# A routed expert layer on one core: the first tile of each expert shrinks from 256 to 128 rows and uses raw fp32 weights

## The reference, cut to what matters

```python
g = jnp.einsum('bsh,ih->bsi', x, gw)
u = jnp.einsum('bsh,ih->bsi', x, uw)
return jnp.einsum('bsi,hi->bsh', jax.nn.silu(g) * u, dw)
...
bids = confidences * wealth
top_bids, selected_experts = jax.lax.top_k(bids, K)      # K = 2 of E = 8
...
x = x + jnp.tanh(g_ffn[0]) * _L0_ffn_ref(_layernorm(x, axis=-1), ...)
```

| expert | 0 | 1 | 2 | 3 | 4 | 5 | 6 | 7 |
|---|---|---|---|---|---|---|---|---|
| rows | 1 | 1 | 272 | 1 | 3820 | 1 | 3 | 4093 |

## Time and profile before

### The profile page before, as it was taken

One profiled execution on the slowest core, in us unless ns is written; L12 is line 12 of the kernel. 1 busy time (PEld: TensorE's weight loads), 2 busy tenths in 40 slices (PEclk: granted clock), 3 DMA queues, 4 the chain that ended last, 5 costly groups with the idle time before them and its releaser, 6 DMA issues.

```text
span 1313.1 us, 25666 instructions
## 1 busy us (share of the span) xinstructions
PE 1158.8 (88%) x9261; PEld 1021.7 (78%) x9261; DVE 672.9 (51%) x1536; ACT 552.5 (42%) x863; POOL 361.3 (28%) x385
## 2 busy tenths in 40 slices
PE   5789888888888888618897999999997999999995
PEld 4556666666666665418897999999997999999995
DVE  2546666666666665445756444444456444444442
ACT  3456565566555554424544232323334323232331
POOL 2112333344334331223534211111133111111111
PEclk7789998999899997758998999999998999999998
DMA  9000111011011100135535321211223222111121
GB/s 319 15 10 26 35 34 33 33 33 38 33 34 42 38 33 27 42 117 200 155 93 157 87 33 29 33 29 24 33 34 114 34 33 33 29 32 30 24 33 24
DMA packets 50753, 73.46 MB, mean 56 GB/s; under 512 B 6288, under 2 KB 42384, under 8 KB 50576
## 3 DMA queue, kind: packets, MB, share of 16 engines
q0 software_dynamic: 20544, 44.05, 14.2%
q1 hardware_dynamic: 29072, 27.65, 7.0%
q10 hardware_dynamic: 1088, 1.11, 0.3%
HBM read 47.11 MB, written 25.43 MB: 55 GB/s over the span
## 4 chain that ended last, share of the span: by engine, by line
PE 44%; DVE 5%; issue 3%; ACT 2%; DMA 1%; POOL 0%; DVEq 0%; POOLq 0%; ACTq 0%
PE gate L1213 15%; PE up L1213 15%; PE down L1229 14%; DVE w_lo L104 4%; ACT h_hi L1273 1%; PE turned L1202 1%; DVE h L1299 1%; ACT w_hi L99 1%; DMA stage<-up_T 1%; DMA out<-y,token 0%; DVE x_lo L1291 0%; DVE h_lo L1301 0%; POOL out L1348 0%; POOL stage L86 0%; DVE y L1314 0%
## 5 line engine op out<-in xcount | busy, mean ns | idle before, releaser
L1348 POOL DMA_INDIRECT out<-y,token x76 | 119.6, 1573 | 495.8 <-DVE y L1314 364.8
L1268 ACT ACTIVATE silu<-gate 128x512 f32<-128x512 f32 x152 | 90.6, 596 | 334.3 <-PE up L1213 334.3
L1299 DVE TENSOR_TENSOR h<-silu,up 128x512 f32<-128x512 f32 x152 | 104.2, 686 | 220.0 <-ACT silu L1268 220.0
L1229 PE MATMUL down<-w_hi,h_hi 128*128 128x256 f32 x608 | 176.4, 290 | 18.4 <-DVE h_lo L1301 18.2
L873 DVE TENSOR_REDUCE max_neg<-maxps 128x4 f32<-128x1024 f32 x128 | 156.4, 1222 | 60.7 <-PE maxps L487 59.1
L1301 DVE TENSOR_TENSOR h_lo<-h,h_hi 128x512 fp32r<-128x512 f32 x152 | 117.9, 776 | 109.6 <-ACT h_hi L1273 109.6
L1229 PE MATMUL down<-w_hi,h_lo 128*128 128x256 f32 x608 | 171.8, 283 | 0.0
L1229 PE MATMUL down<-w_lo,h_hi 128*128 128x256 f32 x608 | 171.5, 282 | 0.0
L675 ACT ACTIVATE probs<-scores 128x1024 f32<-128x1024 f32 x128 | 132.0, 1032 | 90.4 <-PE scores L506 90.3
L1273 ACT ACTIVATE h_hi<-h 128x512 fp32r<-128x512 f32 x152 | 96.0, 631 | 128.7 <-DVE h L1299 128.1
L1213 PE MATMUL gate<-x_hi,w_hi 128*128 128x256 f32 x608 | 125.0, 288 | 12.4 <-issue 7.9
(11 more groups left out here) (153 smaller groups left out, 2162.6 us busy)
## 6 DMA issues: line engine op xcount, KB each, us to landing
xg<-dispatched SPq DMA_DIRECT2D x39, 272.0 KB, 2.8
stage<-gate_T POOLq DMA_DIRECT2D x8, 1024.0 KB, 5.5
stage<-up_T POOLq DMA_DIRECT2D x8, 1024.0 KB, 7.1
stage<-down_T POOLq DMA_DIRECT2D x8, 1024.0 KB, 6.3
x_all<-x SPq DMA_DIRECT2D x16, 256.0 KB, 4.6
ctxT<-ctxT SPq DMA_DIRECT2D x16, 256.0 KB, 2.7
out<-x_all SPq DMA_DIRECT2D x16, 256.0 KB, 2.1
out<-y,token POOLq DMA_INDIRECT x76, 3.8
```

Of the source, the lines that this page charges most:

```text
L1229: last = mm(down[t][:, 0:D], r[:, i, t * P:(t + 1) * P], weights(par, w, 2)[:, i, :], start=i == 0 and m == 0, stop=i == IC - 1 and m == 2)
L1268: nc.scalar.activation(silu[pair % 2][:], gate[pair % 2][:], ACT.Silu).then_inc(s_silu, 1)
L1299: V.tensor_tensor(h[pair % 2][:], silu[pair % 2][:], up[pair % 2][:], ALU.mult).then_inc(s_made, 1)
L1348: pool.indirect_dma_start(out, bass.IndirectOffsetOnAxis(token[:, t:t + 1], axis=0), y[:, t, :], None, compute_op=ALU.add).then_inc(s_adde ...
```

## The change

Each expert's first tile now has 128 rows (`FIRST`) instead of 256, and uses the raw fp32 weights as they land. The tokens are the stationary operand: 8 matmuls of 128 rows by 512 inner columns give `gate` and `up`, two calls of SiLU and two of the product give `h` with rows on partitions, eight transposes (`flip`) and two copies by ScalarE (`hT`) turn it, and 8 matmuls of 256 columns contract it. These are plain fp32 matmuls with one term in place of three. The remaining rows of an expert go through `rest`, tiles of 256 rows with the split weights as before, and their number is now (rows + 127) // 256, which can be 0.

The weights that are split during an expert's first tile are now its *own*, six halves on ScalarE and all six on VectorE, whether or not a `rest` tile follows. There is one pair `w_hi`, `w_lo` instead of two, and three raw buffers instead of one; GpSimd loads the weights of two experts ahead and computes nothing any more. A third of the weights is laid out on the host so that each partition reads one contiguous piece.

```diff
+        def load_third(eng, e, n, to):
+            of = (gate_T, up_T, down_T)[n][e]
+            eng.dma_start(to[:, n * third:(n + 1) * third], of).then_inc(s_stage[e % STAGES][n], 16)
...
-            link(V.tensor_single_scalar(tiles[:], tiles[:], TILE.bit_length() - 1, ALU.arith_shift_right))
-            V.tensor_scalar(tiles[:], tiles[:], 1, None, ALU.max).then_inc(s["counted"], 1)
+            link(V.tensor_scalar(tiles[:], EPILOGUE2.bank("COUNT")[:, 0, 0:EXPERTS], float(TILE - 1 - FIRST), None, ALU.add))
+            V.tensor_single_scalar(tiles[:], tiles[:], TILE.bit_length() - 1, ALU.arith_shift_right).then_inc(s["counted"], 1)
...
+        def over_tiles(eng, name, first, rest, before_rest=None):
+            r = eng.alloc_register(name)
+            eng.reg_mov(r, 0)
             for e in range(EXPERTS):
-                if before_expert:
-                    before_expert(e)
-                tile(e, 0, eng.snap(n), True)
-                eng.reg_add(n, n, 1)
-                count = eng.value_load(tiles[0:1, e:e + 1], min_val=1, max_val=TOKENS // TILE)
-                with eng.If(count > 1):
-                    with eng.Fori(1, count) as j:
-                        tile(e, j, eng.snap(n), False)
-                        eng.reg_add(n, n, 1)
-            return eng.snap(n)
+                before = None if e == 0 else eng.snap(r)
+                first(e, before, 0 if e == 0 else before + e)
+                count = eng.value_load(tiles[0:1, e:e + 1], min_val=0, max_val=TOKENS // TILE)
+                with eng.If(count > 0):
+                    if before_rest:
+                        before_rest(e)
+                    with eng.Fori(0, count) as j:
+                        done = eng.snap(r)
+                        rest(e, j, done, done + (e + 1))
+                        eng.reg_add(r, r, 1)
+            return eng.snap(r)
```

```diff
+            def before_rest(e):
+                for n in range(3):
                     pe.wait_ge(s_split[n], 2 * (e + 1))
...
+            def first_gate_up(e, half, n):
...
+                w = stages[e % STAGES]
+                for mat, bank in ((0, gate[half]), (1, up[half])):
+                    if half == 0:
+                        wait_stage(pe, e, mat)
+                    for c in range(HC):
+                        last = mm(bank[:].rearrange("p a b -> p (a b)"), x_full[:, c, :],
+                                  weights(w, mat)[:, c, half * (INNER // 2):(half + 1) * (INNER // 2)],
+                                  start=c == 0, stop=c == HC - 1)
+                last.then_inc(s_pair, 2)
...
+            def first(e, r, n):
+                pe.wait_ge(s_xlo, n + 1)
+                first_gate_up(e, 0, n)
+                first_gate_up(e, 1, n)
+                flip_h(e, 0, n)
+                turn_rows(n * 16 + 32)
+                wait_stage(pe, e, 2)
+                if not is_zero(n):
+                    pe.wait_ge(s_y, n * TT)
+                first_contract(e, 0, (0, 1))
+                flip_h(e, 1, n)
+                first_contract(e, 0, (2, 3))
+                first_contract(e, 1, range(IC // 2)).then_inc(s_down, 1)
...
             def high_of_rows(done):
                 act.wait_ge(s_turned, done)
+                nc.scalar.activation(x_full[:], turned[:, :, 0:FIRST], ACT.Copy)
                 nc.scalar.activation(x_hi[:], turned[:], ACT.Copy).then_inc(s_xhi, 1)
```

```diff
+                round_weights(*HALVES[:3])
+                first_silu(0)
+                if not is_zero(n):
+                    act.wait_ge(s_down, n)
+                round_weights(*HALVES[3:5])
+                first_silu(1)
+                read_flip(0)
+                round_weights(*HALVES[5:])
+                read_flip(1)
+                high_of_rows(n + 2)
...
+                note_rows(e)
+                rest_of_weights(*HALVES[:2])
+                first_h(0)
+                rest_of_weights(*HALVES[2:4])
+                first_h(1)
+                rest_of_weights(*HALVES[4:])
+                next_rows(r, n, e)
+                V.tensor_scalar(y[:, 0, :], down[0][:, 0:D], weight[:, 0:1], None, ALU.mult).then_inc(s_y, TT)
...
-            def prepare_weights(e):
-                for half in range(2 if e > 0 else 1):
-                    rest_of_weights(pool, e, 0, half, hi[e % 2], lo[e % 2])
-                if e + 1 < EXPERTS:
-                    for n in range(3):
-                        pool.wait_ge(s_split[n], 2 * (e + 1))
-                        load_third(pool, e + 1, n)
...
+            def wait_added(firsts, r, t=0):
...
+            def load_weights(e):
+                for n in range(3):
+                    load_third(pool, e, n, stages[e % STAGES])
+            for e in range(1, STAGES):
+                load_weights(e)
+            def first(e, r, n):
+                if 0 < e and e + STAGES - 1 < EXPERTS:
+                    alone.wait_ge(s_down, n)
+                    for m in range(3):
+                        pool.wait_ge(s_split[m], 2 * e)
+                    load_weights(e + STAGES - 1)
+                pool.wait_ge(s_y, n * TT + TT)
+                if e > 0:
+                    wait_added(e, r)
+                pool.indirect_dma_start(out, bass.IndirectOffsetOnAxis(token[:, 0:1], axis=0),
```

More of the change, by code:

```diff
@@ L73, in build_program @@
         tiles = sb(keep, "tiles", [P, EXPERTS], i32)
-        s_stage = [sem(f"stage_loaded{n}") for n in range(3)]
+        s_stage = [[sem(f"stage{b}_loaded{n}") for n in range(3)] for b in range(STAGES)]
         s_split = [sem(f"weights_split{n}") for n in range(3)]
@@ L1107, in _, with expert_stage @@
             pool.wait_ge(s["scattered"], BATCHES * 16 * 2 * QT)
-def expert_stage(nc, sb_in, sem, load_third, round_weights, rest_of_weights, disp, out, idn, tiles, s_split, s_padded, ROUNDED):
+def expert_stage(nc, sb_in, sem, load_third, disp, out, idn, tiles, stage, s_stage, s_hi, s_split, s_padded):
     with ExitStack() as own:
@@ L1113, in sb @@
             return sb_in(own, name, shape, dt)
-        hi = [sb(f"w_hi{i}", [P, WCOLS], f32r) for i in range(2)]
-        lo = [sb(f"w_lo{i}", [P, WCOLS], f32r) for i in range(2)]
+        stages = [stage] + [sb(f"stage{i}", [P, WCOLS]) for i in range(1, STAGES)]
+        hi = sb("w_hi", [P, WCOLS], f32r)
+        lo = sb("w_lo", [P, WCOLS], f32r)
         xg = sb("xg", [P, TT, ROW])
@@ L1123, in expert_stage @@
         h_lo = sb("h_lo", [P, IC, TILE], f32r)
+        hT = [sb(f"hT{i}", [P, IC // 2, FIRST]) for i in range(2)]
         weight = sb("weight", [P, TT])
@@ L1134, in expert_stage @@
         down = [own.enter_context(nc.psum_tensor(f"down{i}", [P, 512], fp32)) for i in range(TT)]
+        flip = own.enter_context(nc.psum_tensor("flip", [P, IC // 2, FIRST], fp32))
         s_rows = sem("rows_loaded")
@@ L1243, in tile @@
                 turn_rows(n * 16 + 32)
-                contract(e, 2, n, first)
-                contract(e, 3, n, first)
-            def gate_up_split(e):
-                for n in range(2):
+                contract(2, r, n)
+                contract(3, r, n)
+            def before_rest(e):
+                for n in range(3):
                     pe.wait_ge(s_split[n], 2 * (e + 1))
+            def first_gate_up(e, half, n):
+                pe.wait_ge(s_made, n * PAIRS + (half + 1))
+                w = stages[e % STAGES]
[7 more added lines that the diff above has]
+                last.then_inc(s_pair, 2)
@@ new lines, in flip_h, with first_contract @@
+            def flip_h(e, half, n):
+                pe.wait_ge(s_made, n * PAIRS + (2 * half + 4))
+                if 2 * e + half > 0:
+                    pe.wait_ge(s_flipped, 2 * e + half)
+                for i in range(IC // 2):
+                    last = nc.tensor.transpose(flip[:, i, :], h[half][:].rearrange("p a b -> p (a b)")[:, i * P:(i + 1) * P], idn[:])
+                last.then_inc(s_flip, 1)
+            def first_contract(e, half, pieces):
+                pe.wait_ge(s_flipped, 2 * e + half + 1)
+                w = weights(stages[e % STAGES], 2)
+                for i in pieces:
+                    at = half * (IC // 2) + i
+                    last = mm(down[0][:, 0:D], hT[half][:, i, :], w[:, at, :], start=at == 0, stop=at == IC - 1)
+                return last
@@ L1251, in _ @@
             turn_rows(16)
-            over_tiles(pe, "pe_count", tile, gate_up_split)
+            over_tiles(pe, "pe_count", first, rest, before_rest)
         @block.scalar
@@ L1257, in high_of_rows, with rest @@
                 act.wait_ge(s_turned, done)
+                nc.scalar.activation(x_full[:], turned[:, :, 0:FIRST], ACT.Copy)
                 nc.scalar.activation(x_hi[:], turned[:], ACT.Copy).then_inc(s_xhi, 1)
-            def tile(e, j, n, first):
-                def next_weights(n, half):
-                    if first and e + 1 < EXPERTS:
-                        round_weights(act, e + 1, n, half, hi[(e + 1) % 2])
+            def rest(e, j, r, n):
```

(22 more changed lines are left out.)

163 lines of the change are left out of this document (86 added, 77 removed).

## The result

The changed kernel takes 1288.49 us in the median (1285.97 to 1294.51, 5 runs), against 1311.22 before: a ratio of 0.9834, 95% interval 0.981 to 0.9857. It is 22.7 us faster, where 31 were forecast, and lies inside the forecast range. On another chip, in the rounds of later experiments, the ratio was 0.9805 (0.9771 to 0.984).

The account below looks back on a forecast made before the run. TensorE was taken to bound long-expert tiles, weight splitting to lengthen first tiles. 586.2 + 2.6 + 8 x 13.0 + 561.0 + 7.6 + 5.3 + 0.7 = 1267.4 us to the last `down`; predicted median 1280, range 1263 to 1299.

Parts of the forecast that it names:

- Tiles of 256 rows: Expert loops: 32 tiles in place of 38, at 17.53 us each, 561.0 us, with ScalarE's added 0.39 us copy covered.
- TensorE's work and path: 128-row first tile: 12.2 us of TensorE work, 13.0 us with waits; a 512-column instruction bounded by 0.443 and 0.460 us.
- The split beside it: 128-row tile: weight splitting, 9.7 us of ScalarE and 10.4 us of VectorE work, fits within its 13.0 us.
- why the old first tiles were long: Old first tiles: VectorE and GpSimd subtractions colliding on a shared port, one such wait explaining most of an expert's excess; 44.4 us overall.
- Loads: Expert stage: weight and row loads arrive in time, costed at nothing; the first rows might land up to 2.8 us later.
- Start, clock: Expert stage start: first matmul at 586.2 instead of 587.85 us, then 2.6 us lost to TensorE's half-speed clock.
- Boundaries: Between experts: three stalls behind skipped loop code, 7.6 us, slow matmuls after two, 5.3 us, and 0.7 us for handovers.
- Rival (b): More stalls between experts: all five at 3.0 us plus 2.65 of slow clock, 28.3 instead of 12.9; 1296 us, chance 0.14.
- The sum: Last `down` ends at 1267.4 us against 1298.34, 30.9 us less, with what follows unchanged.
- (c): 128-row tile: VectorE or a wait inside the path bounds it at 15.4 us, 19 us more; 1299 us, chance 0.10.
- (e): 128-row tiles: gaps keep TensorE at 1.2 GHz, 90 us more, 1370 us, slower than before; chance 0.04.
- (f): 256-row tiles do not go away: the five small experts run one each, 88 us more, 1368 us; chance 0.02.

Follow-up runs that it names:

- run 7: Changed kernel without splitting the weights of experts 0, 1, 3, 5 and 6, which have no 256-row tile; 1257.26 us, ratio 0.9826 to the kernel before.
- run 5: Kernel before with VectorE subtracting all six halves of the next expert's weights and GpSimd none; 1277.62 us against 1278.0, ratio 0.9982.
- run 8: Changed kernel with two raw weight buffers instead of three; 1256.04 us, ratio 0.9834 to the kernel before.
- run 3: Kernel before with only the expert weights' DRAM layout changed, to 8 KB pieces; 1313.79 us, ratio 1.001.
- run 6: Changed kernel without the 256-row loop code for experts 0, 1, 3, 5 and 6, which skip it; 1239.94 us against 1278.0, ratio 0.9693.
- run 9: The changed kernel itself, measured again on another chip; 1255.83 us, ratio 0.9805 to the kernel before.
- run 1: Changed kernel with the old DRAM layout of the expert weights put back; 1290.27 us, ratio 0.9867 to the kernel before.
- run 12: Kernel before without the loop code for the five experts with one tile; 1271.86 us against 1279.16, ratio 0.9935.
- run 2: Changed kernel with expert 0's weights loaded after the attention's constants arrive; 1279.04 us, ratio 0.9781 to the kernel before.
- run 4: Kernel before with expert 0's weights loaded after the attention's constants arrive; 1303.86 us, ratio 0.9957.
- run 10: Changed kernel with expert 0's weights loaded after the attention's constants, measured beside the changed kernel itself; 1246.68 us, ratio 0.975 to the kernel before.
- run 11: Changed kernel with both the late load of expert 0's weights and no loop code for the five one-tile experts; 1233.11 us, ratio 0.9643 to the kernel before.

## Why the prediction was right, and where it was not

**Tiles of 256 rows.** Right: 32 x 4 SiLUs of 128x512 stand in the loops, a tile takes 17.5 to 17.7 us.

**TensorE's work and path.** Right in kind, 0.8 us too long. An instruction of 512 columns takes 0.43 us, under both of my bounds (0.443 and 0.460). One of 256 columns takes (2.85 - 1.10) / 8 = 0.219 in this tile, where I had 0.230 from the attention. The tile is 12.23 us, not 13.0, with one wait of 0.45 for ScalarE where I had 0.4. An fp32 matmul, which the profile shows as two instructions, is then 0.86 us at 512 columns and 0.44 at 256. The Trainium skill ("FP8 and Floating Point Precision", section "TensorE Precision Notes") has four passes of the array for true fp32. By my estimate, with one column a cycle in each pass, that would be 0.853 and 0.427 us at 2.4 GHz, and the trace agrees at both.

**The split beside it.** Right, and shown by run 7. But the story of *why the old first tiles were long* (the port shared by VectorE and GpSimd) was argued from one row. Run 5 removes the collisions: the waits for `h_lo` fell by 6.1 us and not by most of 44.4, and as the stalls grew, the stage kept its length (710.2 against 709.6 to 711.9). That one engine holds up the other is in the trace (a subtraction of 6.17 us beside GpSimd's, none over 1.226 without them), as the Trainium skill ("SBUF — State Buffer", section "SBUF: two separate sides") has it; that the lock is on that port no run here shows.

**Loads.** Right inside the expert stage (run 8). Wrong in what I left out: the new layout also changes the very first load, expert 0's, which the attention stage issues at 7.4 us and which runs beside that stage's own loads. Over the profiled executions with that early load, the first max-score matmul stands at 38.6 to 42.4 us in all six with 8 KB pieces (changed kernel, runs 3, 6, 7, 8, 9; mean 39.9) and at 33.1 to 37.5 in all four with the old layout (kernel before, runs 1, 5, 12; mean 35.5). That is some 4.4 us. VectorE's wait for the second batch's rows goes the same way: 6.33 to 7.53 us in the six, 1.28 to 3.68 in the four, none in the late loads of runs 2, 4, 10 and 11. The ratios of runs 1 and 3 are too wide to show it in the median, so the size rests on those ten starts alone.

**Start, clock.** The first matmul stands 2.8 us behind the turning instead of 4.6; the forecast had 586.2 - 583.3 = 2.9. And expert 0's tile was 609.56 - 594.71 = 14.85 us, 2.6 over the undisturbed one, as forecast.

**Boundaries.** Right in number, the same three of five; wrong in size. I kept 7.6 us from the kernel before, and they are 3.06 + 4.92 + 5.03 = 13.0, and slow stretches of 1.8, 1.8 and 2.95 instead of two of 2.65. Rival (b) was thus half true: not more stalls, but longer ones. The step that failed is the one that kept the price of a skip because it jumps over the same code. A shorter tile ahead of the jump does not explain the size, for run 5, with old tiles of 19 us and more, had 4.67, 5.64 and 5.74 us at the same boundaries. What goes with the size is the load on the DMA engines. These windows hold nothing but the three stalls of the changed kernel; the column ahead of the last is the DMA share:

```profile
core 0: us, PE busy (x) PEld busy (x) DVE busy (x) ACT busy (x) POOL busy (x), PEclk, DMA share, GB/s
609.56:612.62 3.06, 0.01 (x1) 0.03 (x1) 1.77 (x5) 1.55 (x2) 2.14 (x3) 0.95 0.01 3
669.16:674.08 4.92, 0.00 (x2) 0.03 (x1) 2.98 (x5) 1.55 (x2) 3.31 (x4) 0.97 1.01 420
963.67:968.70 5.03, 0.00 (x2) 0.03 (x1) 2.98 (x5) 1.55 (x2) 2.36 (x1) 0.86 1.00 408
```

And the stall ahead of expert 4 in the kernel before, then in run 5:

```profile
698.56:701.66 3.10, 0.00 (x0) 0.01 (x1) 1.22 (x5) 0.00 (x0) 2.13 (x2) 0.83 0.56 127
```

```profile
663.15:668.79 5.64, 0.00 (x1) 0.01 (x1) 1.22 (x5) 0.00 (x0) 2.28 (x2) 0.92 1.03 399
```

Eleven profiles have such stalls, 33 in all. In the 17 during which GpSimd's queue (the weight loads) took 90% or more of the DMA engines' time, the stall is 4.67 to 6.34 us; in the 16 with 85% or less it is 1.66 to 3.29. In 31 of the 33 a packet of the kind `instruction` moved, and without the five skips six such packets are gone from the page (changed kernel, then run 6; packets, MB, share):

```profile
q8 instruction: 24, 0.39, 0.1%
```

```profile
q8 instruction: 18, 0.29, 0.1%
```

So the forecast step that failed took the price of a skip as fixed, while in the changed kernel the loads of the expert after next run across two of the three boundaries. That the code behind the jump has to be brought in then, and is slower to come beside a full load, fits these stalls, but no run moved the loads alone, so this part is argued.

**The sum.** From the first matmul to the last `down` I had 1267.4 - 586.2 = 681.2 us; it took 1277.07 - 594.71 = 682.4. Tiles 6 us too long and boundaries 6.6 too short made that agreement. That is luck. Of the 8.2 us missing in the total, the stage has 1.0 (29.9 instead of 30.9), the start some 4.4 (layout), the barrier 1.4 and the end 0.9 in this pair (about 0.5 in the mean of all profiles); the rest is within what runs differ. Why the barrier takes 15.4 to 15.5 us in every form of the changed kernel and 14.1 in most of those before (14.9 in run 12) was not tried; the data are the same in all of them, so it goes with the program's code. Rivals (c), (e) and (f) show nowhere: no tile near 15.4 without a stall ahead, the granted clock 0.82 and more, 32 tiles in the loops.

## What to carry to other kernels

When a change touches a load's layout or size, follow every use of that load, the first one at program start above all, where it meets many small loads that stand on the path. When most tiles are nearly empty, a smaller tile in a dearer form wins by what it leaves out, and then the cost at the edges (a jump over code, a cold clock) is the next bound, to be priced in a range and not as it was before; ask what transfers will be under way at that edge. And take a striking row such as a 1.22 us instruction that took 6.17 as a lead to be tested, not as the price of the tile, and when the test shows no gain, look whether another wait has grown by as much.

## What the runs showed of the hardware that I had not expected

A jump over unused loop code cost 1.7 to 6.3 us of TensorE, three times out of five in every kernel that had it, and nothing without it. It was 4.7 us and more exactly where weight loads filled 90% or more of the DMA engines' time. A load of 3 MB at the start of a program, beside some twenty smaller ones, cost 8.6 us of the median in one kernel and 9.2 in the other, in the changed kernel mostly by way of one 256 KB load of rows that landed later. The same kernel differed by 2.6% between two chips (1312.5 and 1278.0 us), and where profiles can be set side by side the difference is in the attention (533.2 us from first max-score matmul to `counts` in one profile, 495.5 in another form of it on the faster chip), with a granted clock of 0.91 there in the first and 0.95 in the second, while the expert stage took nearly the same time (711.9 and 710.2).
